# Attention with a triangular solve on one core: cleared rows, turned outputs in score slots, a separate gather buffer and the last unit's scores inside its solve

## The chip, the cores and the metric

The kernel runs on one core of one Trainium2 chip. The metric is the device time in microseconds, and lower is better. One core has a matrix engine (PE, TensorE), a vector engine (DVE), a scalar engine (ACT), GpSimd (POOL) and the queues that issue DMAs, of which SP's is used most here. The engines run side by side and wait for each other through semaphores.

## The reference

The input is x of 1024 rows (2 sequences of 512) by 256. Four layers follow each other, each x + f(layernorm(x)). The change touches only the first, an attention with 16 heads of 16 columns:

```python
q, k = _rope(q, k)
s = einsum('bihd,bjhd->bhij', k, k) * scale          # strictly lower triangle
p = softmax of s over j < i
L = p * beta
u = solve_triangular(L + eye(T), v, lower=True)
attn = softmax(einsum('bihd,bjhd->bhij', q, k) * scale)   # j <= i
o = einsum('bhij,bjhd->bihd', attn, u) @ Wo
```

The other three layers are a mixture of 64 experts (8 chosen per row), a linear attention with a running sum, and a mixture of 8 experts (2 chosen). They stand behind barriers and are the same in both kernels.

## The kernel before, in words

**Units.** The 16 heads and 2 sequences are worked off in four units u = 0 to 3 (`UNITS`), each 8 heads (`GH`) of one sequence of 512 rows (four tiles of 128, `NI`). Each engine has one hand-written program for the whole stage, and its instructions run in the order written.

**Start** (lines 576 to 603, 884 to 902). SP loads x, constants and weights. DVE computes the layer norm and writes eight tiles AO (line 129 in the helper `dve_norm`). PE turns them (`pe_transposes`, line 146), ACT copies them to xnT, PE projects (`project`, line 293), and DVE rotates and splits into three bf16 parts (`rotate_and_split`). The parts go to DRAM and come back as the stacks `stk["k"]`, `stk["B"]`, `stk["q"]`, two slots each, 96 partitions of data and 32 of extra rows. POOL zeroes the extra rows of both slots (line 889), sets three rows of "B" to one (line 894), and clears `zero`, `XT` and `XR` (lines 896 to 901). XR lies in the buffer of X.

**Maxima and scores.** For each unit DVE takes the maxima of the k and q scores (`maxima`, line 613) from PE's `row_scores` (line 335), which alternate between two slots of the PSUM tile `scores`. The maxima go into the stacks, and `transposed_scores` (lines 349 and 354, c = 0 for keys, 1 for queries, where a mask is added by four more matmuls) makes scores that ACT turns into exps (`exps`, line 806) in EE, one half of which belongs to each unit's parity (`Eu`).

**Solving.** The triangular matrix is inverted in 32x32 diagonal blocks: `gather_blocks` (line 636) collects them from E into Y, half of the 16 copies by DVE (line 643) and half by ACT (line 818), DVE transposes Y to LB (647), sets Y to the identity (648 to 650), `scale` computes -beta/denominator from turned denominators, `invert` (line 674) runs 31 elimination steps on DVE alone, and two transposes give LB and `turned` (706, 707; each counts up `s_y`). Then eight rounds of `sums`, `scaled_sums` and `join` join blocks to 64 and to 128 through the PSUM tile `misc`, with ACT filling XT (`fill_XT`, `joined`) and POOL filling XR (line 920). Between these rounds stand the next unit's row scores and maxima. `solve` (line 430) and `solved` (line 723) then work down the four tiles by turns of PE and DVE; the next unit's key scores are put between the turns (`key_scores`).

**Outputs.** After the solve come the unit's query scores, exps, `attend` (two halves into `misc`), `copy_outputs` on ACT into bankT, `turn_outputs` on PE back into `misc`, and `outputs` on DVE, which divides and writes AO. PE begins the next unit's sums only when both transposes of the inversion are done (`s_y`), the exps are over and both halves of the outputs are written (`s_ao`). The inversion of unit u+1 runs on DVE while PE and ACT make the query exps of unit u.

**SP's queue.** Behind the maxima of a unit it loads the stacks of the unit after the next, when the exps have read the slot, and in between clears rows in DRAM for the second layer. The weight for the outputs (`wo0`, in E) is loaded after the third unit's attention.

## Time and profile before

| | us |
|---|---|
| median of 3 runs | 1138.64 (1136.46 to 1138.84) |
| the profiled execution | 1140.44 |
| its span, first to last instruction | 1138.5 |
| PE busy / DVE / ACT / POOL | 742.7 / 562.3 / 299.1 / 238.5 |
| granted clock of TensorE, mean of the span | 0.799 |

The attention stage is about the first 506 us of the span. A profile row gives its start, its length, the engine, the line of the kernel and the operation; a bracket gives how long the engine was idle before it and which instruction released it. PEclk is the granted clock of PE as a share of full speed. Ends of matmuls are modelled, and rows of several instructions overlap.

### The profile page before, as it was taken

What the parts mean: (1) busy time and instruction counts of PE and PEld (TensorE: products, weight loads), DVE (VectorE), ACT (ScalarE), POOL (GpSimd) and SP (SyncE); (2) the same over time, 40 slices, a digit from 0 to 9 for tenths busy, and PEclk for the clock granted to TensorE, in tenths of its full rate; (3) what the DMA queues carried; (4) which work ended last, traced back from release to release, by engine and by line L of the source; (5) the groups of instructions that cost most, each with busy time, mean ns of one, the idle gap of its engine ahead of it and who ended that gap; (6) DMA issues with size and microseconds to landing.
All of it is one profiled execution on the core that took longest, in us unless ns stands there. A gap on an engine that the chain in (4) does not pass through costs nothing. (4 is left out here: it accounts for less than half of the span.)

```text
span 1138.5 us, 16783 instructions
## 1 busy us (share of the span) xinstructions
PE 742.7 (65%) x6078; PEld 528.0 (46%) x6079; DVE 562.3 (49%) x1556; ACT 299.1 (26%) x494; POOL 238.5 (21%) x251
## 2 busy tenths in 40 slices
PE   1967387777767757762054999998004550999980
PEld 1533264355445436442043999997001240566650
DVE  6796985885788582136300333333346551233322
ACT  1005144442542543311021344443002210211110
POOL 8003002111120210001775000004576005000005
PEclk9897689878979965666576999999556765899995
DMA  3691005122340901017934888886232002111113
GB/s 121 98 138 44 0 3 176 29 32 46 133 57 7 397 12 39 1 49 242 392 130 158 302 297 293 291 291 226 66 100 88 1 0 81 36 43 45 46 37 111
DMA packets 71264, 132.53 MB, mean 116 GB/s; under 512 B 11424, under 2 KB 35360, under 8 KB 70176
## 3 DMA queue, kind: packets, MB, share of 16 engines
q1 hardware_dynamic: 59168, 96.92, 28.9%
q0 software_dynamic: 7680, 20.98, 5.7%
q10 hardware_dynamic: 4352, 13.77, 3.2%
q8 instruction: 41, 0.67, 0.3%
q14 instruction: 23, 0.19, 0.1%
HBM read 77.18 MB, written 54.26 MB: 115 GB/s over the span
## 5 line engine op out<-in xcount | busy, mean ns | idle before, releaser
L1096 PE MATMUL scores<-wgu,zero 128*128 128x192 f32 x512 | 101.7, 345 | 2.7 <-DMA wd<-in_wd 2.7
L806 ACT ACTIVATE E<-scores 128x1280 f32<-128x1280 f32 x64 | 77.0, 1237 | 85.2 <-PE scores L354 54.0
L613 DVE TENSOR_REDUCE block_maxima<-scores 128x10 f32<-128x1280 f32 x64 | 92.3, 1486 | 12.5 <-PE scores L338 11.6
L1197 DVE TENSOR_TENSOR val<-sel,scores 128x192 f32<-128x192 f32 x64 | 22.7, 354 | 149.5 <-ACT sel L1239 149.5
L1253 POOL DMA_INDIRECT expert_rows<-xn_moe,scatter_slots x64 | 62.6, 977 | 133.2 <-DVE gather_slots L1173 114.0
L1096 PEld LDWEIGHTS scores<-wgu,zero 128*128 128x128 f32 x512 | 88.9, 204 | 3.2 <-DMA wd<-in_wd 3.1
L1580 PE MATMUL scores<-w,xgT 128*128 x184 | 88.8, 607 | 0.5 <-issue 0.5
L1089 PE MATMUL misc<-cf,xg 128*128 128x128 f32 x256 | 42.2, 290 | 65.2 <-DMA xg<-expert_rows 65.2
L1230 ACT COPY zero<-misc 128x512 f32<-128x512 f32 x64 | 37.5, 586 | 136.2 <-PE misc L1089 136.2
L911 POOL TENSOR_SCALAR_AFFINE_SELECT E<-E 128x256 f32<-128x256 f32 x64 | 27.0, 447 | 219.4 <-ACT E L806 219.3
L1113 PE MATMUL scores<-wd,slot 96*128 96x256 f32 x256 | 68.2, 391 | 0.5 <-ACT slot L1226 0.5
L1089 PEld LDWEIGHTS misc<-cf,xg 128*128 128x128 f32 x256 | 33.6, 149 | 73.8 <-DMA xg<-expert_rows 36.4
L1189 DVE COPY xnT<-scores 128x512 f32<-128x512 f32 x64 | 44.3, 692 | 28.8 <-PE scores L1113 28.8
L1336 POOL DMA_INDIRECT gb<-expert_outputs,gather_slots x48 | 53.7, 1118 | 22.5 <-issue 13.4
L338 PE MATMUL scores<-cb 128*128 128x128 bf16 x256 | 54.5, 234 | 0.0
L146 PE MATMUL misc<-cf,xn_lin 128*128 128x128 f32 x16 | 3.9, 426 | 77.3 <-DVE xn_lin L129 77.3
L1264 POOL DMA_INDIRECT gb<-expert_outputs,gather_slots x16 | 16.2, 1015 | 168.3 <-DMA expert_outputs<-xnT 163.7
L691 DVE TENSOR_TENSOR tmp<-Y,LB 128x120 f32<-128x120 f32 (+35 forms) x244 | 50.7, 250 | 0.3
L1392 DVE SCALAR_TENSOR_TENSOR X<-gb,w,X 128x256 f32<-128x256 f32 x64 | 29.7, 484 | 42.7 <-DMA gb<-expert_outputs,gather_slots 26.2
L700 DVE TENSOR_TENSOR Y<-Y,tmp 128x120 f32<-128x120 f32 (+35 forms) x244 | 50.7, 250 | 0.1
L1113 PEld LDWEIGHTS scores<-wd,slot 96*128 96x128 f32 x256 | 45.8, 199 | 4.9 <-ACT slot L1226 0.7
L1748 POOL DMA_INDIRECT gb<-sorted_outputs,slots x16 | 16.2, 1014 | 150.7 <-DMA sorted_outputs<-yb 146.1
(232 smaller groups left out, 1526.1 us busy)
## 6 DMA issues: line engine op xcount, KB each, us to landing
expert_rows<-zero SPq DMA_DIRECT2D x32, 512.0 KB, 6.2
xg<-expert_rows SPq DMA_DIRECT2D x64, 256.0 KB, 3.4
expert_outputs<-xnT SPq DMA_DIRECT2D x64, 256.0 KB, 2.9
wgu<-in_wgu SPq DMA_DIRECT2D x32, 384.0 KB, 3.6
w<-in_w ACTq DMA_DIRECT2D x8, 1024.0 KB, 16.5
wd<-in_wd SPq DMA_DIRECT2D x32, 192.0 KB, 3.8
w<-in_w ACTq DMA_DIRECT2D x8, 512.0 KB, 19.0
split_heads<-E SPq DMA_DIRECT2D x8, 384.0 KB, 4.6
```

The costliest lines, as they stand in the source:

```text
L338: ins = nc.tensor.matmul(scores[:, slot, o + w - P:o + w], identb, mask[c, it], start=False, stop=True)
L613: nc.vector.tensor_reduce(bm[:, c, h, :], scores[:, slot, 0:WIDE].rearrange("p (a n) -> p a n", n=P), AX.X, ALU.max).then_inc(s_fd, 1)
L691: nc.vector.tensor_tensor(part, Yc[:, x, 0:n, k:k + 1].to_broadcast([P, n, w]), LB[:, k:k + 1, k + 1:SB].to_broadcast([P, n, w]), ALU.mult ...
L700: nc.vector.tensor_tensor(below, below, part, ALU.add).then_inc(s_inv, 1)
L806: nc.scalar.activation(Eu(u)[:, h, :], scores[:, k % 2, 0:WIDE], ACT.Exp, scale=SCALE).then_inc(s_fa, 1)
L1089: ins = nc.tensor.transpose(misc[:, j % 2, c:c + P], xg[:, j, t, k * P:(k + 1) * P], identf)
L1096: ins = nc.tensor.matmul(scores[:, j % 2, t * 2 * F0:(t + 1) * 2 * F0], xgT[:, j % 2, k, t * P:(t + 1) * P], wgu[:, j // GE, j % GE, k, :] ...
L1113: ins = nc.tensor.matmul(scores[:, j % 2, 1024 + t * D:1024 + (t + 1) * D], hT[:, j % 2, t * P:(t + 1) * P], wd[:, j // GE, j % GE, :], st ...
L1189: nc.vector.tensor_copy(yb[:, j % NY].rearrange("p t d -> p (t d)"), scores[:, j % 2, 1024:1536]).then_inc(s_yv, 1)
L1253: pool.indirect_dma_start(out=xbuf, out_offset=bass.IndirectOffsetOnAxis(ap=isc[:, t, k:k + 1], axis=0), in_=xn[:, t, :], in_offset=None, ...
L1336: pool.indirect_dma_start(out=gb[:, g % NG, :], out_offset=None, in_=ybuf, in_offset=bass.IndirectOffsetOnAxis(ap=ig[:, t, k:k + 1], axis= ...
L1580: ins = nc.tensor.matmul(scores[:, j, g * F1:(g + 1) * F1], xgT[:, j, k, :], w13[:, bass.ds(e, 1), k, g * F1:(g + 1) * F1].rearrange("p e ...
```

## The change

- **Cleared rows.** The extra rows of slot 0 are zeroed by DVE, before its wait for x, instead of by POOL. POOL does slot 1, sets the rows of ones as 2,048 f32 words that hold two bf16 ones each, instead of 4,096 bf16 elements, clears `zero`, and clears XR and XT after the norm's tiles (XR first).
- **Gather.** Blocks are gathered in `turned` instead of Y, 12 by DVE and 4 by ACT. Y is set to the identity by `identity_blocks`: for unit 0 before the first rotation, for the others in the first step of the solve before, after R is copied.
- **Turned outputs.** `turn_outputs` writes to the score slots instead of `misc`, both halves after the second `attend`. ACT copies the second half to bankD. DVE's `outputs` of unit u is done half by half after scaled sums 0 and 1 of unit u+1. PE's sums wait for the first transpose only, the second is waited for before the first join, and the row scores 0 and 1 wait for the outputs that lie in their slots.
- **Last solve.** In the last unit the query scores stand between the turns of the solve (`beside`), and their exps go to the half of E that is free (`Eq`). Afterwards come both attends and the outputs. `wo0` lies in LB and is loaded when the last sums are done.

```diff
+TWO_ONES = 1.0 + 0x3F80 / 2 ** 23
-            wo0 = EE[:, 0, 0, 0:KT * D].rearrange("p (k n) -> p k n", k=KT)
+            wo0 = LB[:].rearrange("p c e -> p (c e)")[:, 0:KT * D].rearrange("p (k n) -> p k n", k=KT)
+            def Eq(u):
+                return EE[:, u % 2] if u + 1 < UNITS else EE[:, (u + 1) % 2]
...
             def diagonal_block(u, s, it):
...
-                return (Y[rows].rearrange("p i (h t) -> p h i t", t=NI)[:, :, :, it],
+                return (turned[rows].rearrange("p i (h t) -> p h i t", t=NI)[:, :, :, it],
...
+            def upper_rows(c, u):
+                return stk[c][KR:P, u % 2].rearrange("p h n -> p (h n)").bitcast(F32)
...
+                    def beside(u, heads):
+                        if u + 1 < UNITS:
+                            key_scores(u + 1, heads)
+                        else:
+                            pe.wait_ge(s_ml[1], 48 * (u + 1))
+                            for h in heads:
+                                transposed_scores(u, 1, h)
...
                     def solve(u):
...
-                                if not last:
-                                    key_scores(u + 1, [2 * it + 1])
+                                beside(u, [2 * it + 1])
...
-                            if not last:
-                                if it < NI - 1:
-                                    key_scores(u + 1, [2 * it + 2] if it else [0, 1, 2])
-                                else:
-                                    denominators(u + 1)
+                            if it < NI - 1:
+                                beside(u, [2 * it + 2] if it else [0, 1, 2])
+                            elif not last:
+                                denominators(u + 1)
                     def turn_outputs(u, hh):
                         pe.wait_ge(s_oc, 2 * u + hh + 1)
+                        pe.wait_ge(s_fa, use(1, u) + GH)
+                        of = bankD if hh else bankT
-                            ins = nc.tensor.transpose(misc[:, hh, it * P:(it + 1) * P], bankT[:, it * P:(it + 1) * P], identf)
+                            ins = nc.tensor.transpose(scores[:, hh, it * P:(it + 1) * P], of[:, it * P:(it + 1) * P], identf)
...
-                        pe.wait_ge(s_y, 2 * (u + 1))
-                        if u:
-                            pe.wait_ge(s_fa, use(1, u - 1) + GH)
-                            pe.wait_ge(s_ao, 2 * u)
-                        else:
+                        pe.wait_ge(s_y, 2 * u + 1)
+                        if u == 0:
                             pe.wait_ge(s_vc, 1 + NT)
                             sums(u, q)
+                            if q == 1:
+                                pe.wait_ge(s_y, 2 * (u + 1))
...
                                 for m in maxima_due(q):
+                                    if u and m < 2:
+                                        pe.wait_ge(s_ao, 2 * u - 1 + m)
...
                         solve(u)
+                        if last:
+                            pe.wait_ge(s_uv, 4 * (u + 1))
+                            attend(u, 0)
+                            attend(u, 1)
+                            turn_outputs(u, 0)
+                            turn_outputs(u, 1)
+                            break
...
-                            if h == 6:
-                                turn_outputs(u, 0)
                         attend(u, 1)
+                        turn_outputs(u, 0)
                         turn_outputs(u, 1)
...
@@ the program of DVE @@
+                    for c in ("B", "k", "q"):
+                        ins = nc.vector.memset(upper_rows(c, 0), 0.0)
+                    ins.then_inc(s_z0, 1)
                     dve.wait_ge(s_x, 16)
...
+                    def identity_blocks():
+                        link(nc.vector.memset(Y[:], 0.0))
+                        nc.vector.memset(flat[:, 0:SB * SB - 1].rearrange("p (a b) -> p a b", b=SB + 1)[:, :, 0], 1.0)
+                        link(nc.vector.memset(flat[:, SB * SB - 1:SB * SB], 1.0))
+                    identity_blocks()
                     for w in range(5):
                         rotate_and_split(w)
...
-                        for s in range(2, P // SB):
+                        for s in range(1, P // SB):
...
-                        link(nc.vector.transpose(LB[:].rearrange("p j i -> p i j"), Y[:]))
-                        link(nc.vector.memset(Y[:], 0.0))
-                        nc.vector.memset(flat[:, 0:SB * SB - 1].rearrange("p (a b) -> p a b", b=SB + 1)[:, :, 0], 1.0)
-                        link(nc.vector.memset(flat[:, SB * SB - 1:SB * SB], 1.0))
+                        link(nc.vector.transpose(LB[:].rearrange("p j i -> p i j"), turned[:]))
...
                                 nc.vector.tensor_copy(r, v).then_inc(s_r, 1)
+                                if u + 1 < UNITS:
+                                    identity_blocks()
...
                             scaled_sums(u, q)
+                            if u and q < 2:
+                                outputs(u - 1, q)
...
-                        outputs(u)
+                    outputs(UNITS - 1, 0)
+                    outputs(UNITS - 1, 1)
...
@@ the program of ACT @@
-                        nc.scalar.activation(Eu(u)[:, h, :], scores[:, k % 2, 0:WIDE], ACT.Exp,
+                        to = Eq(u) if c else Eu(u)
+                        nc.scalar.activation(to[:, h, :], scores[:, k % 2, 0:WIDE], ACT.Exp,
-                        for s in range(2):
+                        for s in range(1):
...
-                            act.wait_ge(s_ot, 2 * u + 1)
-                        nc.scalar.copy(bankT[:], misc[:, hh, :]).then_inc(s_oc, 1)
+                            act.wait_ge(s_dt, min(u + 2, UNITS))
+                        nc.scalar.copy((bankD if hh else bankT)[:], misc[:, hh, :]).then_inc(s_oc, 1)
...
-                        act.wait_ge(s_s, 3 * (u + 1))
+                        if u + 1 < UNITS:
+                            act.wait_ge(s_s, 3 * (u + 1))
...
@@ the program of POOL @@
-                    for u in range(2):
-                        for c in ("B", "k", "q"):
-                            zero_rows(c, u)
-                        link(nc.gpsimd.memset(stk["B"][KR:KR + 3, u], 1.0))
-                        nc.gpsimd.sem_inc(s_ones, 1)
+                    for c in ("B", "k", "q"):
+                        zero_rows(c, 1)
+                    one_rows(1)
+                    pool.wait_ge(s_z0, 1)
+                    one_rows(0)
...
-                    link(nc.gpsimd.memset(XT[:], 0.0))
-                    nc.gpsimd.sem_inc(s_z, 1)
                     pool.wait_ge(s_xn, NT)
                     link(nc.gpsimd.memset(XR, 0.0))
+                    nc.gpsimd.sem_inc(s_z, 1)
+                    link(nc.gpsimd.memset(XT[:], 0.0))
...
@@ the program of SP @@
-                    sp.wait_ge(s_o, 2 * (UNITS - 1))
+                    sp.wait_ge(s_tt, 8 * UNITS)
                     sp.dma_start(wo0, a["wo0"].rearrange("(k p) n -> p k n", p=P)).then_inc(s_wol, 16)
-                    sp.wait_ge(s_tt, 8 * UNITS)
```

## Rows read from the trace of the kernel before

**Rows 1.** Busy time in stretches: PE, PEld, DVE, ACT, POOL, granted clock, DMA, GB/s.
```profile
142.00:447.00 305.00, 224.45 (x3406) 153.19 (x3405) 217.22 (x645) 133.54 (x167) 38.52 (x59) 0.82 0.31 87
...
274.00:293.00 19.00, 14.57 (x209) 8.33 (x213) 5.82 (x18) 10.17 (x10) 6.12 (x16) 0.91 0.87 251
...
447.00:469.00 22.00, 14.89 (x175) 8.68 (x171) 5.69 (x17) 0.00 (x0) 0.00 (x0) 0.50 0.00 1
```

**Rows 2.** Timeline of POOL, the start: start us, us, line, operation.
```profile
11.92 1.80 POOL L889 MEMSET stack_k<- 32x2048 f32 x1
...
15.67 3.54 POOL L894 MEMSET stack_B<- 3x4096 bf16 x1
```

**Rows 3.** Timeline of DVE, the start.
```profile
6.44 2.71 DVE L121 BATCH_NORM_STATS2 stats<-X 128x6 f32<-128x256 f32 x8 [5.17 <-DMA X<-in_x]
...
11.77 13.33 DVE L129 TENSOR_SCALAR AO<-X,mv,rstd 128x256 f32<-128x256 f32 x8
```

**Rows 4.** Line 129 by tile: duration ns min/median/max, first and last start us.
```profile
L129 DVE TENSOR_SCALAR AO<-X,mv,rstd x8: 395/1578/3748, 11.8 to 24.7; 128x256 f32<-128x256 f32 x8
L129 DVE TENSOR_SCALAR xn_moe<-X,mv,rstd x8: 401/404/412, 510.5 to 512.8; 128x256 f32<-128x256 f32 x8
```

**Rows 5.** Timeline of PE: first matmul behind the transposes, in this and the next norm.
```profile
27.15 10.02 PE L293 MATMUL scores<-xnT,E 128*128 128x512 f32 x16 [0.67 <-ACT xnT L153]
...
515.46 3.79 PE L1071 MATMUL scores<-gate,xnT 128*128 128x64 f32 x32 [0.68 <-ACT xnT L153]
```

**Rows 6.** Timelines of DVE and PE around unit 1's gather, and unit 0's first solve step.
```profile
197.86 2.17 DVE L643 COPY Y<-E 32x256 f32<-32x256 f32 x8
201.85 1.97 DVE L647 STREAM_TRANSPOSE LB<-Y 128x1024 f32<-128x1024 f32 x1 [1.82 <-ACT Y L818]
204.10 0.91 DVE L648 MEMSET Y<- 128x1024 f32 x1 [0.28 <-DVE LB L647]
205.11 0.08 DVE L649 MEMSET Y<- 128x31 f32 x1
...
205.44 0.18 DVE L656 TENSOR_SCALAR den<-scores 128x32 f32<-128x32 f32 x1
...
203.29 0.60 PE L380 MATMUL scores<-cf,bankD 128*128 128x128 f32 x4
...
180.33 0.42 DVE L739 COPY bankT<-misc 128x256 f32<-128x256 f32 x1 [1.23 <-PE misc L457]
```

**Rows 7.** Timelines of DVE behind the inversion of unit 1, and of PE in unit 3's joins.
```profile
230.43 1.86 DVE L707 STREAM_TRANSPOSE turned<-Y 128x1024 f32<-128x1024 f32 x1
...
233.29 0.42 DVE L756 TENSOR_TENSOR AO<-misc,rec 128x256 f32<-128x256 f32 x1
235.00 0.86 DVE L718 TENSOR_TENSOR xnT<-misc,ng 32x256 f32<-32x256 f32 x2 [1.28 <-PE misc L403]
...
431.63 1.97 PE L399 MATMUL misc<-X,E 64*64 64x64 f32 x16 [0.71 <-ACT XT L824]
```

**Rows 8.** Timeline of DVE: first and last step of unit 1's solve, then of the last.
```profile
275.24 0.42 DVE L739 COPY bankT<-misc 128x256 f32<-128x256 f32 x1 [1.06 <-PE misc L457]
...
292.50 0.42 DVE L739 COPY bankT<-misc 128x256 f32<-128x256 f32 x1 [0.77 <-PE misc L457]
...
447.97 0.42 DVE L739 COPY bankT<-misc 128x256 f32<-128x256 f32 x1 [4.87 <-PE misc L457]
...
467.70 0.42 DVE L739 COPY bankT<-misc 128x256 f32<-128x256 f32 x1 [1.20 <-PE misc L457]
468.91 0.29 DVE L743 COPY xnT<-misc 128x128 f32<-128x128 f32 x1 [0.78 <-PE misc L468]
```

**Rows 9.** Timeline of PE: the last attend, and the transposes of the result.
```profile
484.55 4.49 PE L478 MATMUL misc<-E,xnT 128*32 128x512 f32 x32 [1.33 <-ACT E L806]
...
491.67 3.82 PE L146 MATMUL misc<-cf,AO 128*128 128x128 f32 x16 [0.81 <-DVE AO L756]
```

**Rows 10.** DMA issues of the first 40 us: count, KB each, median us to landing.
```profile
bb<-in_bb SPq DMA_DIRECT2D x1, 8.0 KB, 7.3
```

**Rows 11.** Groups by form of PE in 467 to 492: count, busy us, mean ns, idle.
```profile
L354 PE MATMUL scores<-cb 128*128 128x128 bf16 x32 | 7.0, 255 | 0.0
```

46 lines of the change are left out of this document (24 added, 22 removed).

## The prediction

> **What bounds the kernel now.** I read the page's slices first, then the engines' timelines of the first 530 us (the change touches only the attention stage), then the waits. No engine is full: in the 305 us from 142 to 447 PE is busy for 224 us at a granted clock of 0.82 [rows 1]. What sets the end is a chain that hops from engine to engine, so I followed the hops and asked at each place that the diff touches which wait ends last. Five places:
>
> 1. The start. The eight tiles of the normalised input (L129) take 13.33 us, each up to 3.7 us. Beside them POOL clears buffers in memsets of 1.80 to 3.54 us [rows 2, 3]; the same eight tiles later, with POOL idle, take 0.40 us each [rows 4]. So a tile waits for a memset of POOL. PE's transposes follow the tiles, and the first projection starts at 27.15 [rows 5].
> 2. The gather of the next unit's blocks (three times, at the end of a solve): DVE's eight copies 197.86 to 200.03, ACT's eight until about 201.8, so DVE waits 1.82 for ACT; then the block transpose, the reset of Y and only at 205.44 the denominators' scaling [rows 6]. The inversion, DVE alone, hangs on it.
> 3. The passage from an inversion to the joins: the last transpose ends at 232.29, then DVE writes the outputs, PE's first sums wait for that (the wait on `s_ao`), and DVE's first scaled sum, which idled 1.28 for them, is at 235.00 [rows 7].
> 4. The last unit's solve: 447.97 to 468.91, PE at 0.50 granted, which is the 1.2 GHz level; unit 1's solve, with next unit's scores in between, runs at 0.91, mostly 2.4 GHz [rows 1, 8].
> 5. The tail: only after that solve come eight heads of scores and exps, attention, outputs, until PE's transposes of the result start at 491.67 [rows 9].
>
> **The change, part by part.**
>
> *Start.* POOL keeps three clearings (1.80 each, 0.83 to about 6.4), two row-settings of 2,048 f32 in place of 4,096 bf16 elements (3.54 [rows 2]; half the elements, 1.8), and `zero` (0.96, estimated as L648's 1,024 elements). It is done near 11.4, before the tiles start at 11.77. XR and XT come after the tiles: 5.7 us, until about 21; beside them DVE has the cast and the new identity, both needed only after the first projection (above 24), so nothing waits for them. The tiles then take 2.7 instead of 13.33. DVE gets three clearings of 2,048 elements. The nearest row is the memset of 1,024: the row says 0.91, the reset that follows it starts 1.01 later [rows 6]; so 2.02 each, 6.1 in all, from 1.3 to 7.4. X is there at 6.44 [rows 3], so the norm starts 0.9 later (bounds 0.3 by the bare row's length, 1.4). The Trainium skill (VectorE: DVE Perf Modes, Zero memsets can be issued as uint32) gives a memset one cycle per element whatever the type, and the clock of its table makes that 2.13 us each, 0.3 us more in all; the row's length is below that rule, the spacing near it. The sum goes by the spacing. Tiles start at 12.7; in the same sequence of the next norm the tiles start at 510.5 and the first matmul behind the transposes at 515.46, 4.95 later [rows 4, 5]; the last weights are issued by about 6 and land 7.3 later, by 13.4 [rows 10], as the first two tiles are done. First projection: 12.7+4.95 = 17.7, **9.4 earlier** (bounds 8.4 and 12.4: the first projection runs at 1.2 GHz, and could be partly faster once transposes and matmuls are dense).
>
> *Gather.* DVE copies 12 blocks (0.27 each by 2.17/8: 3.3 us), ACT 4 (half of its 4.0, no longer last). The transpose starts 0.6 earlier, and the reset of Y (1.1) is gone from here, so DVE would be ready 1.7 earlier. What is late next: the turned denominators, PE 203.29 to 203.89 [rows 6]. Scaling starts at about 203.95 instead of 205.44: **1.5, three times, 4.5**. For the first unit PE's denominators are last by far: 0. The identity (1.1 us) moves to the solve's first step, where DVE idles 1.23 [rows 6]: at most 0.1 lost; the first one is in the shadow of the projection.
>
> *Joins.* Sums need only the first of the two transposes, DVE goes from the second straight to the scaled sums: 232.3 instead of 235.00, **2.7** for units 1 and 2. The outputs (the second half's product 0.42, up to 233.71 [rows 7]; with the reciprocal and gaps 0.75 each half) now follow scaled sums 0 and 1, where DVE idles about 1.28 for PE [rows 7]: cost 0 (all in the open: 1.5 per unit). Queued behind them are the row scores, that wait for the outputs' two counts; by the old timing they need the slots 0.7 and more after the outputs are done. In the last unit ACT's copies of XT release the second level (431.63 [rows 7]); ACT starts at the same transpose as before and gains only its own idle: 1.7 (between 0 and 2.7). Sum **7.1** (between 2.6 and 8.1). With the third block, PE also doesn't stand 1.8 us for turning the first half; this only moves slack before the inversion's end, and brings the loads of the stacks 1.5 forward, so that they stay ahead of the row scores by what they had.
>
> *Last solve.* Eight heads go between its steps, exps to the other half of E. Unit 1's solve has the same pattern: 275.24 to 292.50, 17.3 us, against 447.97 to 467.70, 19.7, without heads at the low clock [rows 8]. The four masks of a head add 0.2 (at most 7.0/8 = 0.9 [rows 11], where the matmuls overlap; I take a quarter), some of it hidden, and the first three heads will still be at the low clock: together 1.9 over unit 1, in the middle between nothing and the 3.5 of three wholly slow and open heads. I take 19.2: **0.5 gained** (bounds: 2.4 gained, 8.9 lost).
>
> *Tail.* Now 469.2 to 491.67, 22.5. After: two attends (4.49 at the low clock [rows 9], half at the high), I take one of each, ACT's copy 0.7, turning 1.1, outputs 0.9, hops 0.3: 9.8. **12.7 gained** (10.7 to 14.9).
>
> Everything after (projection of the outputs, three later stages) starts behind a barrier and moves as a whole; the weight for the outputs is now loaded at the end of the last joins and wanted a solve and a tail, some 30 us, later: hidden. Sum: 9.4+4.5+7.1+0.5+12.7 = **34.2**. The profiled execution took 1140.44 (span 1138.5, 1.94 around it); it stands 1.8 above the median 1138.64. So 1106.2 for this execution, **1104.4** against the median. About 0.2% (2.3 us) is what a measurement can tell from no change.
>
> **The rivals.**
>
> *A. DVE's clearings queue behind POOL's, as the tiles do.* Alternating, three of 2.0 and three of 1.8 end at 12.3 instead of 7.4, so the norm is 4.9 later than I take: 1109.3. For it: the tiles [rows 2, 3]. Against: a tile reads and writes SBUF, a memset only writes, and no row shows a memset of DVE that waited. The Trainium skill (SBUF — State Buffer, Who interferes with whom) says that a DVE instruction with at most one SBUF input outside the 2-port modes doesn't contend, and the other kind is blocked for the whole of the other's instruction; by that rule A does not happen. Chance 0.10.
>
> *B. The heads in the last solve are not hidden.* Its steps are round trips PE-DVE-PE of half a microsecond's idle, and a head is about 1 us at the high, 1.5 at the low clock. If PE stays at 0.50 as now [rows 1], I estimate three heads at 4.4 at once and five at 0.9 each in the steps, and both attends are slow: 8.9 lost, 10.7 gained in the tail, so 22.8 in all: 1115.8. The skill (TensorE: Matmul & The Clock Gate, HAM oscillation — how this bites in real kernels) says that pauses in the stream put the array back on the low clock, which would give B's time. Unit 1's solve with its heads at 0.91 speaks against it here. Chance 0.13.
>
> *C. The joins' gain doesn't come:* DVE bounds those stretches, and the outputs come back in it (1.5 a unit), or the row scores wait for them: 2.6 instead of 7.1, 1108.9. Here the change would not do what it says. Chance 0.05.
>
> *D. Slower: PE falls to its low level in the whole of the middle.* The units are laid out on a PE that is at 0.82 granted, 224 busy of 305 us [rows 1]. Work there is then 224x0.82 = 184 at full clock; the new stretch has some 293 us, and to lose the 34 us it must grow to 327: PE full at a granted clock of 0.56. At 0.50 the work alone is 367 us, 74 more than 293: about 1178. It decides from 0.56 down. For it: the last unit runs at 0.50. Against: nothing leaves PE in units 0 to 2. Chance 0.02.
>
> **How the numbers follow.** The forecast has 0.70, and its own bounds are 1100 to 1109 (start +3/-1, joins, solve and tail by halves of their bounds). The range takes in A, C and the nearer part of B (heads partly hidden): 1098 to 1115. All but D is faster by tens of microseconds: faster 0.97, within 0.2% 0.01, slower 0.02.
>
> **What would show it.** Right: tiles of 0.4 us, first projection near 17.7, DVE's scaling about 1.5 after the gather's transpose without a reset of Y; first scaled sum directly behind the second transpose; exps of the last unit inside the solve, the result's transposes within 10 us of its end. Wrong: a late norm (A), a last solve of 27 us at 0.50 (B), reductions of the maxima later against the scaled sums (C), more than 1 us before the row scores of head 0 (stacks late).

## The result and the profile after

| | before | after |
|---|---|---|
| median (lowest to highest), us | 1138.74 (1136.46 to 1140.22) | 1099.03 (1098.32 to 1104.98) |
| the profiled execution, us | 1140.44 | 1104.98 |
| its span | 1138.5 | 1103.1 |
| PE busy / DVE / ACT / POOL, us | 742.7 / 562.3 / 299.1 / 238.5 | 719.3 / 561.9 / 291.1 / 231.2 |
| granted clock, mean of the span | 0.799 | 0.809 |

The ratio is 0.9667, with its interval 0.9635 to 0.9699: 39.7 us less by the medians. The profiled execution of after is the slowest of the six on record (the other spans lie between 1096.4 and 1101.6), so between the two profiles there are only 35.4. The engines are not busier for it: the change takes waits out of a chain, and that is how the two traces are best compared. I noted in both where each unit of the attention stage passes the same points: DVE's scaling of the denominators, its first scaled sum, the copy of R behind the inversion, the last output. Subtracting neighbours gives the length of each step.

| step | before | after | gained |
|---|---|---|---|
| span's start to unit 0's R | 178.87 | 167.69 | 11.18 |
| R to scaling (gather), units 1 / 2 / 3 | 26.57 / 26.60 / 26.65 | 25.06 / 25.50 / 25.54 | 1.51 / 1.10 / 1.11 |
| scaling to first scaled sum, units 1 / 2 / 3 | 29.56 / 29.53 / 29.56 | 26.91 / 26.89 / 26.92 | 2.65 / 2.64 / 2.64 |
| scaled sums to R (joins), units 1 / 2 / 3 | 38.95 / 36.24 / 20.34 | 36.24 / 36.26 / 21.37 | 2.71 / -0.02 / -1.03 |
| last R to last output (solve, attention) | 48.73 | 31.89 | 16.84 |
| last output to the next norm | 14.93 | 11.47 | 3.46 |
| **attention stage** | 506.53 | 461.74 | **44.79** |
| the rest of the span | 632.0 | 641.4 | **-9.4** |

*The start.* POOL's timeline of after: start, length, then engine, line and operation, in brackets the idle time and who ended it. It answers to [rows 2].

```profile
6.40 1.80 POOL L933 MEMSET stack_B<- 3x2048 f32 x1
...
10.30 0.96 POOL L941 MEMSET zero<- 128x1024 f32 x1 [0.15 <-POOL stack_B L933]
...
15.89 2.15 POOL L944 MEMSET X<- 128x2048 f32 x1 [4.63 <-DVE AO L131]
```

The memset of one rows has half the length of that in [rows 2], POOL is done at 11.26, and XR is cleared only when DVE's tiles release it. DVE's timeline, against [rows 3]:

```profile
1.75 1.76 DVE L607 MEMSET stack_B<- 32x2048 f32 x1 [0.48 <-DVE R L605]
3.89 1.76 DVE L607 MEMSET stack_k<- 32x2048 f32 x1 [0.38 <-issue]
6.03 1.76 DVE L607 MEMSET stack_q<- 32x2048 f32 x1 [0.38 <-issue]
7.82 2.71 DVE L123 BATCH_NORM_STATS2 stats<-X 128x6 f32<-128x256 f32 x8
...
13.16 2.67 DVE L131 TENSOR_SCALAR AO<-X,mv,rstd 128x256 f32<-128x256 f32 x8
```

The eight tiles take 2.67 us instead of 13.33. The three clearings start 2.14 apart, though each row says 1.76; the norm's first instruction follows 1.79 behind the start of the third, at 7.82, so the norm is 1.4 late, not 0.9. PE's timeline shows what comes of it, against 27.15 in [rows 5]:

```profile
14.04 3.79 PE L148 MATMUL misc<-cf,AO 128*128 128x128 f32 x16 [14.04 <-DVE AO L131]
18.51 8.78 PE L303 MATMUL scores<-xnT,E 128*128 128x512 f32 x16 [0.68 <-ACT xnT L155]
...
443.62 4.51 PE L495 MATMUL misc<-E,xnT 128*32 128x512 f32 x64 [0.38 <-DVE xnT L778]
...
453.56 7.17 PE L597 MATMUL misc<-LB,xnT 128*128 128x256 f32 x32 [0.68 <-ACT xnT L155]
466.53 3.82 PE L148 MATMUL misc<-cf,xn_moe 128*128 128x128 f32 x16 [5.79 <-DVE xn_moe L131]
471.02 7.09 PE L1115 MATMUL scores<-gate,xnT 128*128 128x64 f32 x32 [0.68 <-ACT xnT L155]
...
892.22 7.00 PE L1594 MATMUL misc<-gate,xnT 128*128 128x8 f32 x32 [0.67 <-ACT xnT L155]
```

The lower part is the tail, the result's projection and two stretches behind the attention. Both attends are one row of 64 matmuls in 4.51 us, as long as 32 of them in [rows 9], so all ran at the high level. The last two rows are the same work as in before, but longer: the router's 32 matmuls take 7.09 against 3.79 [rows 5], those of the last stage 7.00 against 4.11. The row of the last stage in the kernel before:

```profile
930.91 4.11 PE L1550 MATMUL misc<-gate,xnT 128*128 128x8 f32 x32 [0.67 <-ACT xnT L153]
```

*The gather, the joins and the solve* on DVE's timeline of after, to be laid beside [rows 6], [rows 7] and [rows 8]:

```profile
186.67 3.25 DVE L678 COPY turned<-E 32x256 f32<-32x256 f32 x12
189.95 1.99 DVE L682 STREAM_TRANSPOSE LB<-turned 128x1024 f32<-128x1024 f32 x1
...
192.75 0.19 DVE L689 TENSOR_SCALAR den<-scores 128x32 f32<-128x32 f32 x1 [0.48 <-PE scores L390]
...
217.75 1.88 DVE L740 STREAM_TRANSPOSE turned<-Y 128x1024 f32<-128x1024 f32 x1
219.66 0.86 DVE L751 TENSOR_TENSOR xnT<-misc,ng 32x256 f32<-32x256 f32 x2
220.84 0.42 DVE L790 TENSOR_TENSOR AO<-scores,rec 128x256 f32<-128x256 f32 x1
221.72 0.86 DVE L751 TENSOR_TENSOR xnT<-misc,ng 32x256 f32<-32x256 f32 x2 [0.46 <-PE misc L413]
...
423.47 0.42 DVE L774 COPY bankT<-misc 128x256 f32<-128x256 f32 x1 [4.86 <-PE misc L475]
428.35 0.29 DVE L778 COPY xnT<-misc 128x128 f32<-128x128 f32 x1 [4.45 <-PE misc L485]
...
443.27 0.29 DVE L778 COPY xnT<-misc 128x128 f32<-128x128 f32 x1 [0.53 <-PE misc L485]
```

Read in it: the transpose starts with no idle time behind the twelve copies; the scaling waits 0.48 for PE's turned denominators (L390) and for nothing else; the first scaled sum starts 0.03 after the second transpose, and the output's product sits between two scaled sums, where DVE idled. In the last solve the first step stands 4.86 for PE, as it did before (4.87 [rows 8]), and the second 4.45, because three heads of scores lie in between; it still ends at 443.56, 25.2 us behind the copy of R at 418.38.

The stretches of after that the text comes back to, as windows (the stretch and its length, busy time of PE, PEld, DVE, ACT and POOL, granted clock, DMA share, GB/s): the first projection in two parts, units 0 to 3, the joins of the last unit, its solve, the attends, and the second norm with the router.

```profile
18.50:22.00 3.50, 3.49 (x5) 1.54 (x6) 0.00 (x0) 0.00 (x0) 3.21 (x1) 1.00 0.00 0
22.00:27.50 5.50, 5.50 (x14) 2.45 (x13) 3.28 (x6) 0.00 (x0) 0.00 (x0) 1.00 0.00 0
...
132.00:428.00 296.00, 216.32 (x3387) 152.43 (x3425) 220.53 (x655) 128.60 (x157) 37.42 (x59) 0.83 0.32 90
...
397.00:418.00 21.00, 16.91 (x393) 16.25 (x394) 7.17 (x16) 13.22 (x18) 2.13 (x2) 0.50 0.01 2
...
423.00:443.00 20.00, 15.37 (x226) 10.54 (x222) 5.60 (x16) 9.90 (x8) 0.00 (x0) 0.87 0.01 2
443.00:450.00 7.00, 5.99 (x74) 2.78 (x72) 1.36 (x5) 1.17 (x2) 0.00 (x0) 1.00 0.00 0
...
461.00:478.00 17.00, 10.80 (x48) 9.90 (x48) 6.42 (x26) 5.21 (x7) 0.00 (x0) 0.63 0.36 108
```

The middle is at 0.83 as in [rows 1]. The last joins are at 0.50, the last solve, at 0.50 before, is at 0.87, and the attends run wholly at the high level. Within the solve, the stretch from 418.4 to 428 is still at 0.50, with the first three heads in it, and the rest from 428 to 443.5 at 1.00.

### The profile page after: what moved, and what is told of

It reads as the page before. It is cut to its first block and busy times, and to the rows that moved or that the text cites. A ratio compares the mean times of both kernels' runs of the same rounds, so it can differ in the third digit from the quotient of the medians.

```text
span 1103.1 us, 16757 instructions
## 1 busy us (share of the span) xinstructions
PE 719.3 (65%) x6034; PEld 522.6 (47%) x6079; DVE 561.9 (51%) x1575; ACT 291.1 (26%) x478; POOL 231.2 (21%) x248
## 5 line engine op out<-in xcount | busy, mean ns | idle before, releaser
L1274 ACT COPY zero<-misc 128x512 f32<-128x512 f32 x64 | 37.4, 585 | 136.9 <-PE misc L1133 136.9
L1380 POOL DMA_INDIRECT gb<-expert_outputs,gather_slots x48 | 55.2, 1150 | 22.5 <-issue 13.4
L413 PE MATMUL misc<-LB,E 32*32 32x32 f32 x512 | 17.6, 231 | 45.6 <-DVE LB L739 37.9
```

The lines of the kernel that those rows point to most:

```text
L1380: pool.indirect_dma_start(out=gb[:, g % NG, :], out_offset=None, in_=ybuf, in_offset=bass.IndirectOffsetOnAxis(ap=ig[:, t, k:k + 1], axis= ...
```

## The experiments

All times below are against the kernel before on the same chip, whose medians were 1139.80 to 1140.73, except where said. Where a step is named, its length is taken from the landmarks of the table above.

Two comparisons are given, and they differ. By the ratios, the start put back costs 12.4 us, the outputs first 4.3, the gather put back 10.0 and the heads behind 11.7 (differences to after's 0.9667, times 1138.74). The interval of outputs first, 0.9677 to 0.9733, overlaps that of after, 0.9635 to 0.9699; the other three lie clear of it. By the ends of the attention stage in the traces it is 8.2, 7.4, 8.5 and 11.4. Each trace is one execution, and in these kernels stretches that no edit touches differ between traces: unit 0's scaling starts between 101.4 and 103.8 us in the nine traces that share after's start, and what follows the attention stage takes 632.0 us in the trace of before and 634.6 to 641.4 in those of the changed kernels on the faster chips without added matmuls there, with after's the longest.

### The start put back

```diff
-                    for c in ("B", "k", "q"):
-                        ins = nc.vector.memset(upper_rows(c, 0), 0.0)
-                    ins.then_inc(s_z0, 1)
...
-                    for c in ("B", "k", "q"):
-                        zero_rows(c, 1)
-                    one_rows(1)
-                    pool.wait_ge(s_z0, 1)
-                    one_rows(0)
+                    for u in range(2):
+                        for c in ("B", "k", "q"):
+                            zero_rows(c, u)
+                        link(nc.gpsimd.memset(stk["B"][KR:KR + 3, u], 1.0))
+                        nc.gpsimd.sem_inc(s_ones, 1)
```

XT's clearing stands ahead of the wait for the tiles again.

> Undone: only the part at the start (POOL clears both slots, rows of ones as bf16, XT before the norm). My theory, that the parts add: tiles of the norm 13 us again, first projection near 27.2, first rotation on DVE near 33.8 (9.8 later than in the changed kernel), and R of unit 0 11.2 later, since PE's matmuls up to the row scores then run later on the high clock; the whole about 1110. Rival: of the 11.2 only 8.6 (the projection's start) belong to this part and the rest came from elsewhere: 1107.5.

Measured: 1113.5, ratio 0.9776 (0.9748 to 0.9804). In the trace the first rotation is 8.4 us later and the attention stage ends 8.2 later, with each step between as in after. Line 131's group of the first norm in the trace of this kernel (shortest, median and longest of the eight, in ns, and the stretch):

```profile
L131 DVE TENSOR_SCALAR AO<-X,mv,rstd x8: 396/1491/3749, 12.1 to 24.7; 128x256 f32<-128x256 f32 x8
```

The tiles are again up to 3.75 us with POOL's memsets beside them, and 0.40 without. So the start is worth 8.2 in the trace and 12.4 by the ratios, and what it gains is the tiles. Even so, unit 0's R stands at 175.95, 2.9 before its place in the trace of before: that part of the table's 11.18 is not the start's edit. The first rotation alone stands at 33.78 in the trace of before and at 32.36 in this one, with the projection starting at 27.15 in both.

### The start alone, in the kernel before

The same edit the other way round: the kernel before, with the clearings of slot 0 on DVE, the rows of ones as f32, and XR and XT behind the tiles.

```diff
+                    for c in ("B", "k", "q"):
+                        ins = nc.vector.memset(stk[c][KR:P, 0].rearrange("p h n -> p (h n)").bitcast(F32), 0.0)
+                    ins.then_inc(s_z0, 1)
```

> The kernel before with only the part at the start. Theory that the parts add: the first rotation near 24 instead of 33.8 and R of unit 0 between 8.2 and 11.2 earlier than before (8.2 is what undoing it cost in the changed kernel), all behind it unchanged: 1129 to 1131. Rival: what comes earlier is partly eaten by a later wait for the DMAs of the stacks or by the clock: above 1133.

Measured: 1130.14, ratio 0.992 (0.9894 to 0.9947), 9.7 less than 1139.80: clear of no change, and inside what was forecast. In its trace R of unit 0 is 13.4 earlier than in that of before, the attention stage ends 18.0 earlier, and 8.3 of that are lost again behind the stage. It also answers a question that I had not put to it. Two windows of its trace, over the joins of unit 1 and of unit 2 (length, then busy time of PE, PEld, DVE, ACT and POOL, granted clock, DMA share, GB/s):

```profile
222.00:258.00 36.00, 29.39 (x551) 23.36 (x546) 31.45 (x43) 12.18 (x20) 0.00 (x0) 0.91 0.01 3
...
314.00:353.00 39.00, 32.85 (x563) 25.91 (x558) 31.35 (x43) 12.53 (x20) 0.05 (x1) 0.83 0.01 3
```

The same windows of the kernel before:

```profile
235.00:274.00 39.00, 32.39 (x546) 25.58 (x546) 31.75 (x45) 11.97 (x20) 0.00 (x0) 0.83 0.01 3
...
330.00:366.00 36.00, 29.24 (x547) 23.26 (x545) 31.54 (x44) 12.08 (x20) 0.00 (x0) 0.91 0.01 3
```

Between scaled sums and R a unit takes 36.2 or 39.0, the longer one with the granted clock at 0.83 in place of 0.91 and some 3 us more of PE. In the kernel before that hit unit 1, in this one unit 2, and in after none, with the same instructions. (There is a length between: unit 0 takes 37.2 to 37.4 here and in nine other traces.) Also the stretch from the last output to the next norm is 11.47 here, though the tail is that of before (14.93), and that tail itself, from the last R to the last output, takes 47.0 here where it took 48.73. So the 2.71 of unit 1's joins and the 3.46 behind the last output, in the table above, are not the change's.

### The outputs ahead of the scaled sums

```diff
                         if u == 0:
                             pe.wait_ge(s_vc, 1 + NT)
+                        else:
+                            pe.wait_ge(s_ao, 2 * u)
...
+                            if u and q == 0:
+                                outputs(u - 1, 0)
+                                outputs(u - 1, 1)
                             scaled_sums(u, q)
-                            if u and q < 2:
-                                outputs(u - 1, q)
```

> Undone: only the order in the joins (DVE writes both halves of the outputs before the first scaled sum, and PE's first sums wait for them). My theory: each passage is 2.65 us longer, less 1.0 in the last unit, together 7.0: about 1106. Rival C: the outputs cost the same wherever they stand, since DVE bounds the joins: 1099 to 1100. Open in both: unit 1's joins took 34.5 us before and 31.8 after from R to R counted from the first maxima; if that dip of PE's clock hangs on the pause before the sums, it comes back here (2.7 more).

Measured: 1106.57, ratio 0.9705 (0.9677 to 0.9733). DVE's timeline of this kernel, in unit 1:

```profile
217.45 1.86 DVE L742 STREAM_TRANSPOSE turned<-Y 128x1024 f32<-128x1024 f32 x1
...
222.01 0.86 DVE L753 TENSOR_TENSOR xnT<-misc,ng 32x256 f32<-32x256 f32 x2 [1.29 <-PE misc L413]
```

This is the pattern of [rows 7], idle time included: from scaling to scaled sum 29.56 again in place of 26.9. The last unit gives 1.1 back (20.29 in place of 21.37). Its own steps are thus 6.9 longer. The attention stage ends 7.4 later, but that these agree is in part luck: the joins of units 0 to 2, which this edit could only shorten, are 2.9 longer in all in this trace, and other steps 2.4 shorter. By the ratios the edit costs 4.3, with intervals that overlap; what shows the gain is the wait that comes and goes in the trace.

### The gather put back

`diagonal_block` reads Y, DVE copies 8 blocks and ACT 8, and `identity_blocks` stands behind the block transpose.

```diff
-                        for s in range(1, P // SB):
+                        for s in range(2, P // SB):
...
-                        link(nc.vector.transpose(LB[:].rearrange("p j i -> p i j"), turned[:]))
+                        link(nc.vector.transpose(LB[:].rearrange("p j i -> p i j"), Y[:]))
+                        identity_blocks()
```

> Undone: only the gather (blocks into Y, 8 by DVE and 8 by ACT, identity written behind the transpose). My theory: the scaling of units 1 to 3 starts 1.5 later after R, less 0.4 that the identity in the solve's first step costs units 2 and 3: 1.1 to 1.5 each, 3.7 in all: about 1103. Rival: the identity in the solve delays its first step by all its 1.1 us and the gain is nearly nothing: 1100.

Measured: 1111.22, ratio 0.9755 (0.9725 to 0.9785). DVE's timeline in unit 1:

```profile
187.51 2.18 DVE L677 COPY Y<-E 32x256 f32<-32x256 f32 x8
191.50 1.99 DVE L681 STREAM_TRANSPOSE LB<-Y 128x1024 f32<-128x1024 f32 x1 [1.82 <-ACT Y L854]
193.77 0.91 DVE L619 MEMSET Y<- 128x1024 f32 x1 [0.28 <-DVE LB L681]
...
195.11 0.18 DVE L689 TENSOR_SCALAR den<-scores 128x32 f32<-128x32 f32 x1
```

The wait for ACT and the reset are back, and R to scaling takes 27.06, 27.41 and 26.61 where after has 25.06, 25.50 and 25.54: 2.0, 1.9 and 1.1, so 5.0. The stage ended 8.5 later, though. The rest are joins that were 1.0, 1.2 and 2.7 longer, less 1.4 at the start and in the tail; unit 2's joins, the longest, took 38.95 with its window at a granted clock of 0.84.

So one trace alone would have put 8.5 on the gather; its own steps say 5.0 (3.7 by after against before). The two differ because the step from R to scaling holds a solve, and its first matmuls (L475, 16 of them) run at either level. Here are those of unit 1 in this kernel, and DVE's copy that waits for them:

```profile
260.13 1.08 PE L475 MATMUL misc<-XT,R 128*32 128x128 f32 x16 [0.35 <-ACT mrow L836]
...
261.28 0.42 DVE L772 COPY bankT<-misc 128x256 f32<-128x256 f32 x1 [1.58 <-PE misc L475]
```

They take 1.08 us in units 0 and 1 of this kernel and 0.65 in unit 2; in after 0.79 in unit 0 and 1.08 in units 1 and 2. With them at 1.08 the copy starts 1.81 behind R without the identity and 1.88 with it. Like compared with like, R to scaling is 27.06 and 27.41 against 25.50 and 25.54, and, in the units where they are short, 26.61 against 25.06: 1.5 to 1.9 us a unit.

### The heads behind the last solve, and the same with idle matmuls

`beside` does nothing in the last unit; the eight heads of scores come behind the solve, ahead of both attends.

```diff
-                        else:
-                            pe.wait_ge(s_ml[1], 48 * (u + 1))
-                            for h in heads:
-                                transposed_scores(u, 1, h)
...
                         if last:
+                            pe.wait_ge(s_ml[1], 48 * (u + 1))
+                            for h in range(GH):
+                                transposed_scores(u, 1, h)
                             pe.wait_ge(s_uv, 4 * (u + 1))
```

> Undone: only the last solve (its query scores stand behind it; the outputs still go to the score slots, both attends after all heads). My theory: the last solve runs at a granted clock of 0.50 again, 21 us, and the tail is 15 longer, and the transposes and the projection of the result lose about 3 us of the high clock: 20 in all, about 1119. Rival: the clock has no part in it, only the moved heads: 8 heads at 1.5 (bounded by the exps) less what they cost inside the solve: 12 to 13 us, 1112.

Measured: 1111.96, ratio 0.977 (0.9732 to 0.9807). From R to the last output 42.68 us in place of 31.89, 10.8 more; the kernel before took 48.73.

The second kernel has, besides, four matmuls per head between the turns of the solve, which write scores that nobody reads (idle matmuls, in what follows), so that PE is as dense there as in after while the real heads still come behind.

> As the kernel with the heads behind the last solve, but in the solve, in place of each head, PE runs four matmuls of the same shape (without masks) whose results nobody reads. It separates the clock from the moved work. My theory: the matmuls keep PE at 2.4 GHz, so the last solve keeps the length it has with the heads inside (R to the end of the outputs 42.7 without them, with them some 2 less), and the heads behind still cost their 11: the outputs end near 40.5 after R, so the time is 1110, near that of the kernel without dummies. Rival: most of the gain of the last part is the clock: near 1103.

Measured: 1109.4, ratio 0.9735 (0.9716 to 0.9755). R to the last output: 38.69. The dense stream gives back 4.0 of the 10.8: that is the clock's share. PE's clock goes with it: from R to the last U's copy the granted clock is 0.80 here, 0.81 in after and 0.50 with nothing between the turns. The other 6.8 come from the moved work, scores and exps that lie beside the solve. And from 48.73 to 42.68, 6.0 us, is what the rest of the tail's rewriting gives by the trace of before: both attends without a turn and a copy between them. Against the 47.0 that the same tail took in the kernel with the start alone it is 4.4.

### Heads divided around the first attend

The real heads behind the solve once more, but the first half is attended after head 5, with ACT's copy after head 6, as the kernel before had it, and both turns at the end.

```diff
+                            transposed_scores(u, 1, 0)
+                            pe.wait_ge(s_uv, 4 * (u + 1))
+                            for h in range(1, GH):
+                                transposed_scores(u, 1, h)
+                                if h == 5:
+                                    attend(u, 0)
+                            attend(u, 1)
...
-                            if h == 6 and u + 1 < UNITS:
+                            if h == 6:
                                 copy_outputs(u, 0)
```

> As the kernel with the heads behind the last solve, but the first attend stands behind the sixth head, as it did before; the turned outputs stay in the score slots. It tells where the rest of the tail's gain is from: before, R of unit 3 to the end of the outputs took 48.7 and from there to the second norm 14.9; with all heads, then both attends, 42.7 and 11.5. My theory: it is PE's pause of 1.3 to 1.8 us between the attends that put it back on 1.2 GHz (the second attend 4.5 instead of 2.3, the transposes and half of the projection slow): so here 46 to 47 and 14.9: the time 1118. Rival: the gain is from the turning in the score slots, which PE no longer waits for: 42 to 43 and 11.5, 1112.

Measured, on another chip whose kernel before takes 1168.13: 1142.63, ratio 0.9783 (0.9755 to 0.9811). R to the last output is 46.11. PE's timeline shows the two attends, with two heads and a wait for the exps between them:

```profile
453.07 2.36 PE L501 MATMUL misc<-E,xnT 128*32 128x512 f32 x32
...
459.25 4.03 PE L501 MATMUL misc<-E,xnT 128*32 128x512 f32 x32 [2.18 <-ACT E L855]
```

Putting the attends together behind all heads is thus worth 3.4 (46.11 to 42.68). 1.8 of it is the second attend, 4.03 for half of 4.51: the pause did put it down, as the theory says. What remains, 2.6 against the trace of before and 0.9 against that of the start alone, is left to the turn and the outputs of the first half, that are no longer on the way; no run isolates it. That the order of the tail stretches what follows it fell: with it, the last output to the next norm still takes 11.46. By its ratio the time would be 1114 against 1138.74, between the 1118 of the theory and the 1112 of the rival.

### Clearing q's rows later

DVE clears B and k ahead of x and q behind the masks' cast; PE's scores wait for all three.

```diff
-                    for c in ("B", "k", "q"):
-                        ins = nc.vector.memset(upper_rows(c, 0), 0.0)
-                    ins.then_inc(s_z0, 1)
+                    for c in ("B", "k"):
+                        nc.vector.memset(upper_rows(c, 0), 0.0).then_inc(s_z0, 1)
...
                     nc.vector.sem_inc(s_cb, 1)
+                    nc.vector.memset(upper_rows("q", 0), 0.0).then_inc(s_z0, 1)
```

> The changed kernel, but DVE clears the rows of the q stack only behind the cast, when it would idle for the projection, and not before the norm. The profile of the changed kernel shows the clearings 2.14 apart and the norm 1.4 late. If each clearing takes 2.14 of DVE's time whatever POOL does, two end at about 6.0, the norm starts with x at 6.4 and everything is 1.4 earlier: the first rotation 1.4 earlier, 1097.6. Rival: the spacing comes from POOL's memsets beside them (contention), or the time of the first rotation hangs on the clock: no difference in the whole.

Measured: 1097.51, ratio 0.9623 (0.9603 to 0.9642), a median 1.5 below that of after, and inside what a measurement can tell. PE's timeline of its start:

```profile
12.98 3.83 PE L148 MATMUL misc<-cf,AO 128*128 128x128 f32 x16 [12.98 <-DMA bb<-in_bb]
17.48 9.51 PE L303 MATMUL scores<-xnT,E 128*128 128x512 f32 x16 [0.68 <-ACT xnT L155]
```

The norm starts with x, at 6.43, and the tiles 1.4 earlier. Then the transposes wait for the weights' DMA at 12.98, and the first projection starts 1.03 earlier and takes 9.51 in place of 8.78, since more of it runs at the low level. The first rotation is 0.30 earlier in this trace. So of the 1.4 that the clearings still cost, a DMA takes 0.4, and the clock most of the rest. But 0.30 says little: with the projection starting at 18.51 or 18.52, as in after, the first rotation stands anywhere from 22.32 to 24.64 in the other traces. Nor does this trace show a gain at the end of the stage (462.17 against 461.74). Its shorter span lies behind it, where the last stage's router, which no edit touched, takes 4.21 for after's 7.00:

```profile
889.60 4.21 PE L1595 MATMUL misc<-gate,xnT 128*128 128x8 f32 x32 [0.68 <-ACT xnT L155]
```

That clearing q's rows later gains anything is not shown.

### Matmuls ahead of the router

The 9.4 us that after loses behind the attention stage are partly in the router's matmuls, that come after 5.8 us of norm without PE. Eight matmuls whose result nobody reads go there:

```diff
+                    for i in range(8):
+                        nc.tensor.matmul(scores[:, 1, 0:512], onesb, cb[:, 0:512], start=True, stop=True)
                     pe_transposes(pe, 2, xn, xn_ready(pe, 1))
```

> The changed kernel with eight matmuls of 128 by 512 that nobody reads, in front of the transposes of the second norm, where PE idles 5.8 us. In the changed kernel the router's matmuls there take 7.1 us, before they took 3.8, which is the clock at its low and its high level. My theory: the loss of 3.7 us behind the attention is that clock; with dummies the router takes 3.8 again and the stretch from the norm to the maxima 12.8 instead of 16.4: 3.7 us faster. Rival: the level follows something else than PE's work of the last microseconds: no change.

Measured: 1097.31, ratio 0.9619 (0.9595 to 0.9643). PE's timeline:

```profile
464.55 1.89 PE L1111 MATMUL scores<-cb 128*128 128x512 bf16 x8 [1.01 <-PEq L289]
469.33 2.70 PE L148 MATMUL misc<-cf,xn_moe 128*128 128x128 f32 x16 [2.90 <-DVE xn_moe L131]
472.71 4.79 PE L1117 MATMUL scores<-gate,xnT 128*128 128x64 f32 x32 [0.68 <-ACT xnT L155]
```

Transposes 2.70 for 3.82 and router 4.79 for 7.09; from the norm to the maxima 12.98 for 16.41. The window from 461 to 478 of this kernel, against 0.63 in after's:

```profile
461.00:478.00 17.00, 11.78 (x68) 8.87 (x66) 8.39 (x30) 5.21 (x7) 0.00 (x0) 0.92 0.37 108
```

The mechanism is shown in the trace, 3.4 us: of the traces without matmuls there, eleven have 16.4 for this stretch and that of before 12.75, and both with them have 13.0. The median moves by 1.7, about the resolution.

### Matmuls in the last joins

The last unit's joins run wholly at 0.50. Two matmuls of 512 columns behind each round were to lift that.

```diff
+                            if last:
+                                for i in range(2):
+                                    nc.tensor.matmul(scores[:, 1, 1024:1536], onesb, cb[:, 0:512], start=True, stop=True)
```

> The changed kernel, with two matmuls of 128 by 512 that nobody reads behind every round of the last unit's joins, where PE runs at a granted 0.50 from 397 to 423. If PE's level bounds these rounds and the extra work lifts it, R of unit 3 comes 3 to 5 us earlier after the first scaled sum (21.4 now) and the first three heads of the solve 1.5: 1094 to 1095. Rival: the extra work costs its own time at the low level, 8 times 0.9 less the pauses it fills: 2 to 4 slower.

Measured, on the other chip (before 1168.13): 1131.77, ratio 0.9683 (0.9652 to 0.9715). The window of that unit's joins in this kernel, of which the same stretch stands above for after:

```profile
397.00:423.00 26.00, 25.02 (x414) 18.90 (x414) 7.61 (x17) 13.19 (x19) 1.98 (x2) 0.50 0.02 3
```

PE is busy for 25.0 of 26 us and the clock stays at 0.50. The added matmuls are simply paid, 4.1 us (25.43 for 21.37). In this stretch a busy PE did not bring the high level.

### The changed kernel again, on the other chip

> The changed kernel itself, for how its stretches vary from run to run: from the first rotation to the scaling of unit 0 79.3 in one profile, 77.9 to 81.5 in variants that don't touch it; joins of 36.2, in some variants one of them 37.2 or 39.0. My theory: PE's level falls in and out of these by chance, so the unforecast 2.7 us in unit 1 is no gain of the change, and a second profile of the same kernel differs by 1 to 5 us in just such steps: 1099 to 1101. Rival: the steps are fixed for a kernel, and the stretches come out as in the first profile within 0.2.

Measured: 1127.4 (1126.18 to 1132.58), ratio 0.9651 (0.9627 to 0.9675), within its interval the 0.9667 measured first. A window of its trace, over the joins of unit 0:

```profile
132.00:171.00 39.00, 32.48 (x546) 25.67 (x546) 31.70 (x45) 13.37 (x21) 0.87 (x1) 0.83 0.01 3
```

This time unit 0 is the slow one, of the very kernel that had none in its first trace (36.2 there). Which unit it hits thus differs between two executions of one kernel, here on two chips. The routers do not differ between these two: 7.09 and 7.0 in both. Of the other chip's extra 28 us, 18 lie in the experts' gathered rows: from the first to the last that DVE adds up it is 91.7 us here and 74.0 in the first trace.

### The best version

q's rows late, and twelve idle matmuls ahead of the transposes of the router's norm and of the last stage's.

```diff
+                    for i in range(12):
+                        nc.tensor.matmul(scores[:, 1, 0:512], onesb, cb[:, 0:512], start=True, stop=True)
                     pe_transposes(pe, 4, xn, xn_ready(pe, 3))
```

> The changed kernel with the q rows cleared behind the cast, and twelve matmuls nobody reads before the transposes of the second norm and of the last stage's norm, where the router's matmuls take 7 us at the low level. If the three gains add (0.3 to 1.4, 3.4, 3 to 4), the ratio to the kernel before falls from 0.966 by 7 to 9 us to about 0.959. Rival: PE's level by chance gives that back elsewhere, and the ratio is that of the kernel with the first dummies alone, 0.962.

Measured: 1094.99 (1093.36 to 1096.18), ratio 0.9604 (0.9591 to 0.9618), 4.0 below after's median and its range and interval wholly below after's. The interval overlaps that of the kernel with the first idle matmuls alone (0.9595 to 0.9643), so that the gains add is not shown. PE's timeline:

```profile
460.12 2.75 PE L1112 MATMUL scores<-cb 128*128 128x512 bf16 x12 [1.01 <-PEq L289]
...
468.27 4.77 PE L1118 MATMUL scores<-gate,xnT 128*128 128x64 f32 x32 [0.68 <-ACT xnT L155]
...
884.11 4.15 PE L1599 MATMUL misc<-gate,xnT 128*128 128x8 f32 x32 [0.68 <-ACT xnT L155]
```

Both routers are at their short time, 4.77 and 4.15, where after's profile has 7.09 and 7.00. For the first, two traces with the idle matmuls stand against eleven at 7.09 without. For the last stage they are not shown to be the cause: its router took 4.14 to 4.40 in five kernels that have none there (heads behind, heads with idle matmuls, heads divided, q's rows later, matmuls ahead of the router), and 7.0 in seven.

## Why the prediction was right, and where not

The time fell inside the range, 5.4 us below the forecast of 1104.4. The mechanism held at all five places; two sizes were off, and some differences that cancel are luck. Step by step, from the profiled executions:

| term | forecast | trace | undone, end of the stage |
|---|---|---|---|
| start | 9.4 | 8.6 at the first projection, 11.2 at unit 0's R | 8.2 |
| gather | 4.5 | 3.7 | 8.5, own steps 5.0 |
| joins | 7.1 | 6.9 | 7.4, own steps 6.9 |
| last solve and tail | 0.5 + 12.7 | 16.8 | 11.4 for the heads alone |
| behind the attention | 0 | -9.4 | |

**Start.** The mechanism was right: tiles of 0.4 us, projection at 18.51 for a forecast 17.7. Three clearings put the norm 1.4 late instead of 0.9, and that is mostly where the first one starts: at 1.75, not 1.3. From there to the norm it is 6.07, for the 6.1 of the sum, but made up otherwise: two spacings of 2.14 instead of 2.02, and 1.79 from the third to the norm. The other 0.4 of the projection's 0.8 lies between the tiles and it (5.35 for 4.95), where the transposes take 3.79 and took 3.46 in the next norm of before. The Trainium skill (VectorE: DVE Perf Modes, Zero memsets can be issued as uint32) gives one cycle per element, by its table's clock an estimate of 2.13. The spacing of 2.14 between two clearings is near that, but the trace does not bear it out as the time that one occupies: the row is 1.76, the norm followed 1.79 behind, and for the 1,024 elements of Y the next instruction starts 1.00 later, where an estimate by that rule is 1.07. The measurement decides. The steps from there to unit 0's R were 2.5 shorter, and with the start put back they were again 2.9 shorter than before: that is no work of this edit.

**Rival A** fell. The memsets of DVE beside POOL's kept their rows of 1.76, and that of Y has the same 0.91 beside POOL's clearing of XR (16.70 in after) as with POOL idle [rows 6], while tiles beside POOL's memsets stretched to 3.75. The Trainium skill (SBUF — State Buffer, Who interferes with whom) says that a DVE instruction with at most one SBUF input outside the 2-port modes does not contend, and for the memsets these rows bear it out.

**Gather.** The limit named, PE's turned denominators, is the one that the trace shows (0.48 idle for L390). Unit 1 gained 1.51 as forecast; units 2 and 3 only 1.1. The difference of 0.4 falls to the solve's first step, where the identity now stands, but it is PE's level and not the identity: the same step took 1.81 without the identity and 1.88 with it when its matmuls took 1.08. At equal level the gather is worth 1.5 to 1.9 a unit, as forecast or a little more.

**Joins.** 2.65, 2.64 and 2.64-1.03 for forecast 2.7, 2.7 and 1.7. The outputs cost nothing behind the scaled sums, so C fell: undoing that alone brought the 29.56 back.

**Last solve and tail.** I had split this as 0.5 and 12.7. The solve came out as R to the last U's copy at 443.56, 25.2 us, against 26.3 before (442.87 to 469.20): 1.15 gained. The tail gained 15.7 instead of 12.7. The failed estimate is "two attends, one of each level": both were at the high one, 4.51 together for 6.7. The other 0.8 are the turn and the hops. That they are 3.0 and not less hangs on the trace of before; the kernel with the start alone spends 1.7 less in the same tail, so 14.0 to 15.7 is what can be said. The sum's "first three heads at the low clock" was right: until 428 the solve is at 0.50. The solve's 0.87 against 0.50 [rows 1] is what the heads do to the clock, and the idle matmuls put 4.0 of the 10.8 on it. Rival B wanted a PE at 0.50 here, and so fell with it; heads behind the solve came to within 4 us of B's forecast of 1115.8, but by another way. D fell too: the whole middle of after is at 0.83, far above the 0.56 from which it decides.

**"Moves as a whole"** was the sentence that failed. The stages behind the barrier hold the same instructions, but in the profiled execution they took 9.4 more: 3.7 in the router (16.41 for 12.75), 3 in the last stage's norm and router (7.00 for 4.11 is most of it), the rest of 2 to 3 among the experts. Here before's trace was the lucky one: in all eleven other traces without idle matmuls there, that of the kernel before with only the start changed among them, the router's stretch takes 16.4. After's was unlucky in the last stage, which is at 4.1 to 4.4 in five later ones, and its 641.4 is the longest of the faster chips' traces. And before's trace was unlucky in two other places, 2.71 in unit 1's joins and 3.46 behind the last output. My terms sum to 34.2, the same terms in the trace to 38.6, and the medians differ by 39.7. The lucky and unlucky places nearly cancel, so that the time came out this near is luck in part; of what the forecast missed, the tail's level is shown, and the start's 1.8 is not the edit's.

What stays open is why PE falls in one unit's joins or in one router stretch and not in the next. Equal instructions have taken either length, and for a unit's joins one and the same kernel has; whether that is chance or hangs on the time at which a stretch begins, these runs do not tell.

## What to carry to other kernels

Where a chain hops between engines, ask at each hop which of its waits is there only for a shared buffer: giving the turned outputs another place, and the gather another buffer, brought 2.6 and 1.1 to 1.9 us per unit with no instruction less. Independent work between the round trips of a solve pays twice, since it is hidden and keeps TensorE at its high level; idle matmuls helped in that solve too and behind a gap ahead of the router, and not within the small-tile joins, that stayed at the low level with PE busy for 96% of the time. And take a step's length from several executions before you believe a single us: the same joins took 36.2 or 39.0 in one kernel, and idle matmuls ahead of the last stage seemed to work until five kernels without them had the same short time.

## What the runs showed of the hardware

- A DVE memset of 2,048 f32 has a row of 1.76 us. The next memset started 2.14 behind it twice in after and 2.04 in the kernel with q's rows later, the norm's first instruction 1.79 behind it.
- Beside POOL's memsets a DVE tensor_scalar that reads and writes SBUF in f32 stretched from 0.40 to up to 3.75 us; a DVE memset kept its length (1.76; 0.91 for 1,024 with and without POOL).
- The same instructions ran at another granted clock in another trace, in steps worth 2.7 us (joins, one kernel twice), and between kernels that are the same there 3.5 (the result's projection), 3.7 (router) and some 3 (last stage).
- Twelve or eight matmuls of 512 columns ahead of the router lifted it (7.09 to 4.77 and 4.79; the window 0.63 to 0.92); in a stretch of 64 by 64 matmuls, with PE busy for 96%, the clock stayed at 0.50.
- The granted clock is given as 1.00 in both windows of the first projection, though 5 matmuls took 3.5 us in the first and 14 took 5.5 in the second (a few of them the next tile's), and single ones of this line take 1.22 us or 0.59. At the start of this trace the lengths of the matmuls tell the clock, not that column.
